# Both residual subtractions of the recurrent state's half 1 moved from VectorE to GpSimd

## The reference

```python
# layer 0: for each batch row, factors a1, b1, a2, b2 from gelu(LN(cond) @ W1 + bias1) @ W2 + bias2
mid = gelu(x @ base_down + (x @ a2) @ b2.T)
x   = x + (x + mid @ base_up.T + (mid @ b1) @ a1.T)
# layer 1: a recurrence over time, all batch rows together
xW = x @ Wx + b                      # (4, 512, 256)
h  = cond                            # (4, 256)
for t in range(512):
    h = tanh(xW[:, t] + h @ Wh)      # float32
    out[:, t] = x[:, t] + h
```

## Time and profile before

| | |
|---|---|
| Median of 3 runs | 555.61 us (550.74, 555.61, 555.97) |
| The profiled execution | 551.53 us, its span 549.7 us |
| TensorE busy | 511.1 us of the span (93%) |
| VectorE busy | 296.5 us (54%) |
| ScalarE busy | 176.5 us (32%) |
| GpSimd busy | 21.9 us (4%), none after 38.4 us |
| Tanh operations of the recurrence | 1024, from 54.2 to 544.9 us |

### The profile page before, as it was taken

How to read it: one execution, slowest core, us unless ns; L and a number is a source line. 1 busy time by engine, 2 the same in 40 slices (tenths; PEclk the granted TensorE clock), 3 DMA queues, 4 the chain that set the end, 5 groups by cost and what they waited for, 6 DMA issues and landing times.

```text
span 549.7 us, 32433 instructions
## 1 busy us (share of the span) xinstructions
PE 511.1 (93%) x14388; PEld 439.2 (80%) x14388; DVE 296.5 (54%) x2262; ACT 176.5 (32%) x1154; POOL 21.9 (4%) x34
## 2 busy tenths in 40 slices
PE   6988999999999999999998999899999989998995
PEld 4224777899999999999998888888888888888884
DVE  1154666555656555565555555555555555555553
ACT  2010222333333434333333333333333333333322
POOL 2850000000000000000000000000000000000000
PEclk7698999999999999999999999999999999999998
DMA  8950000000000000000000000000000000000000
GB/s 295 383 185 2 3 4 3 13 5 14 4 13 5 14 4 4 16 4 14 4 14 5 14 4 14 4 7 11 5 14 4 13 5 13 4 14 5 8 9 12
DMA packets 11346, 16.01 MB, mean 29 GB/s; under 512 B 1715, under 2 KB 7106, under 8 KB 11202
## 3 DMA queue, kind: packets, MB, share of 16 engines
q1 hardware_dynamic: 10352, 13.37, 7.4%
q10 hardware_dynamic: 854, 0.57, 0.4%
HBM read 11.85 MB, written 2.10 MB: 25 GB/s over the span
## 4 chain that ended last, share of the span: by engine, by line
PE 89%; ACT 5%; issue 2%; DVE 1%; DMA 1%; ACTq 0%; DVEq 0%
PE bank L833 65%; PE bank L762 7%; ACT w_sb L429 5%; PE bank L803 3%; PE bank L808 3%; PE bank L656 2%; PE bank L790 2%; PE bank L649 1%; DMA beta_sb<-in_L_cond_ln_beta 1%; PE bank L771 1%; PE bank L635 1%; PE bank L757 1%; PE bank L671 1%; PE bank L820 1%; PE bank L676 0%
## 5 line engine op out<-in xcount | busy, mean ns | idle before, releaser
L833 PE MATMUL bank<-w_sb,whp 128*128 128x52 bf16 x6132 | 243.0, 186 | 25.1 <-ACT w_sb L429 24.8
L591 DVE TENSOR_TENSOR r_ring<-w_sb 128x4 f32<-128x4 f32 x1022 | 136.5, 163 | 211.6 <-ACT w_sb L429 207.7
L429 ACT ACTIVATE w_sb<-bank 128x4 f32<-128x4 f32 x1024 | 142.0, 173 | 320.8 <-PE bank L833 320.8
L833 PEld LDWEIGHTS bank<-w_sb,whp 128*128 128x128 bf16 x6132 | 188.7, 96 | 68.4 <-ACT w_sb L429 46.4
L833 PE MATMUL bank<-r_ring,whp 128*128 128x52 bf16 x4096 | 219.9, 185 | 0.1
L833 PEld LDWEIGHTS bank<-r_ring,whp 128*128 128x128 bf16 x4096 | 173.9, 96 | 0.2 <-issue 0.2
L833 PE MATMUL bank<-l_ring,whp 128*128 128x52 bf16 (+1 forms) x2048 | 156.4, 177 | 0.0
L596 DVE TENSOR_TENSOR l_ring<-r_ring 128x4 bf16<-128x4 f32 x1024 | 136.3, 162 | 0.0
L833 PEld LDWEIGHTS bank<-l_ring,whp 128*128 128x128 bf16 x2048 | 121.6, 96 | 0.0
L762 PE MATMUL bank<-xp,wxp 128*128 128x32 bf16 x1536 | 71.6, 177 | 0.0
L762 PEld LDWEIGHTS bank<-xp,wxp 128*128 128x128 bf16 x1536 | 54.0, 96 | 0.0
(11 more groups left out here) (109 smaller groups left out, 192.3 us busy)
## 6 DMA issues: line engine op xcount, KB each, us to landing
w_sb<-in_L_cond_W SPq DMA_DIRECT2D x16, 512.0 KB, 10.8
x_sb<-in_x SPq DMA_DIRECT2D x4, 512.0 KB, 11.2
out<-o_sb SPq DMA_DIRECT2D x64, 32.0 KB, 1.6
down_sb<-in_L_cond_base_down SPq DMA_DIRECT2D x1, 256.0 KB, 5.2
w_sb<-in_L_cond_W ACTq DMA_DIRECT2D x1, 256.0 KB, 5.6
up_sb<-in_L_cond_base_up ACTq DMA_DIRECT2D x1, 256.0 KB, 9.0
wx_sb<-in_L_cond_Wx SPq DMA_DIRECT2D x1, 256.0 KB, 10.2
wh_sb<-in_L_cond_Wh SPq DMA_DIRECT2D x1, 256.0 KB, 10.4
```

Source lines behind the costliest of these rows:

```text
L429: nc.scalar.activation(h_ring[:, m, slot(pair, s), 0:B], zt, ACT.Tanh).then_inc(h_ready, 1)
L591: nc.vector.tensor_tensor(r_ring[:, k, q, 0:B], state_before(pair, s, k)[:, 0:B], state_hi_before(pair, s, k)[:, 0:B], ALU.subtract).then_ ...
L833: return nc.tensor.matmul(zbank(p, q, m)[:, col0:col0 + n], whp[part][:, k, P * m:P * (m + 1)], rhs[:, 0:n], start=False, stop=stop, skip_ ...
```

## The change

GpSimd gets a loop over all 512 steps with two subtractions each, r and l of half 1. VectorE keeps r and l of half 0 and its other work. Since two engines now count, `r_ready` and `l_ready` become one semaphore for each half, and TensorE's waits name them. No product, tanh, operand or shape is changed.

```diff
-        r_ready = sem("r_ready")
-        l_ready = sem("l_ready")
+        r_ready = [sem(f"r_ready{k}") for k in range(K2)]
+        l_ready = [sem(f"l_ready{k}") for k in range(K2)]
...
@@ gpsimd, after the memset of line 352 @@
+            def residues(pair, first, last):
+                for s in range(PAIR):
+                    q, step = s % 2, PAIR * pair + s
+                    pool.wait_ge(h_ready, 2 * step + 2)
+                    nc.gpsimd.tensor_tensor(r_ring[:, 1, q, 0:B], state_before(pair, s, 1)[:, 0:B],
+                                            state_hi_before(pair, s, 1)[:, 0:B], ALU.subtract).then_inc(r_ready[1], 1)
+                    pool.wait_ge(r_ready[1], step + 1)
+                    nc.gpsimd.tensor_tensor(l_ring[:, 1, q, 0:B], r_ring[:, 1, q, 0:B], r_hi[:, 1, q, 0:B],
+                                            ALU.subtract).then_inc(l_ready[1], 1)
+
+            over_pairs(residues)
...
@@ vector, residues @@
-                    for k in range(K2):
-                        dve.wait_ge(h_ready, 2 * PAIR * pair + 2 * s + k + 1)
-                        nc.vector.tensor_tensor(r_ring[:, k, q, 0:B], state_before(pair, s, k)[:, 0:B],
-                                                state_hi_before(pair, s, k)[:, 0:B],
-                                                ALU.subtract).then_inc(r_ready, 1)
-                    for k in range(K2):
-                        dve.wait_ge(r_ready, 2 * PAIR * pair + 2 * s + k + 1)
-                        nc.vector.tensor_tensor(l_ring[:, k, q, 0:B], r_ring[:, k, q, 0:B], r_hi[:, k, q, 0:B],
-                                                ALU.subtract).then_inc(l_ready, 1)
+                    step = PAIR * pair + s
+                    dve.wait_ge(h_ready, 2 * step + 1)
+                    nc.vector.tensor_tensor(r_ring[:, 0, q, 0:B], state_before(pair, s, 0)[:, 0:B],
+                                            state_hi_before(pair, s, 0)[:, 0:B], ALU.subtract).then_inc(r_ready[0], 1)
+                    dve.wait_ge(r_ready[0], step + 1)
+                    nc.vector.tensor_tensor(l_ring[:, 0, q, 0:B], r_ring[:, 0, q, 0:B], r_hi[:, 0, q, 0:B],
+                                            ALU.subtract).then_inc(l_ready[0], 1)
...
@@ tensor, recurrence @@
-                    pe.wait_ge(r_ready, done + 1)
+                    pe.wait_ge(r_ready[0], step + 1)
...
-                    pe.wait_ge(r_ready, done + 2)
+                    pe.wait_ge(r_ready[1], step + 1)
                     for part in range(2):
                         product(part, 1, 0, r_hi[:, 1, q, :])
-                    pe.wait_ge(l_ready, done + 1)
+                    pe.wait_ge(l_ready[0], step + 1)
                     product(0, 0, 0, l_ring[:, 0, q, :])
-                    pe.wait_ge(l_ready, done + 2)
+                    pe.wait_ge(l_ready[1], step + 1)
                     product(0, 1, 0, l_ring[:, 1, q, :], stop=True).then_inc(z_ready, 1)
```

More of the change, by code:

```diff
@@ L828, in recurrence @@
                     col0 = B * (s % TS // 2)
-                    done = 2 * PAIR * pair + 2 * s
+                    step = PAIR * pair + s
+                    done = 2 * step
                     def product(part, k, m, rhs, stop=False):
```

## The result

The changed kernel takes 629.64 us as the median of 4 runs (628.97 to 631.24), the kernel before 553.2 us beside it (550.74 to 555.97). The ratio is 1.138, 95% interval 1.134 to 1.143: slower by 14%. The profiled execution took 629.54 us, 78.0 more than the 551.53 before. The ratios in this document leave out executions that were longer at a lower granted clock; only the kernel with two more operations on VectorE had any, three of twelve, at 563 to 566 us.

What follows compares the result with a forecast made beforehand. It took a loop through three engines, 0.943 us a step, as the bound, with half 1's remainders lacking slack. 0.11 us in 478 steps plus twelve partly covered added 53 us to 555.6: 608 predicted, range 592 to 664.

Steps and rivals of the forecast that it cites:

- Rival 1: GpSimd's small subtractions take longer than 172 ns, at most 226 each: up to 104 us, 660; chance 0.18 including times between.
- two signs of being wrong: The GpSimd pair with hand-overs takes other than 0.50 us, or l of half 1 did not release the product.
- What releases the product: l of half 1 releases the product that ends output half 0, with no slack; the competing path is within 0.01 us.
- path B: Tanh of half 1, its r and l, then the 4-column product: 0.453 us from tanh's end, predicted 0.564, 0.11 longer.
- Less VectorE work is worth nothing: Two subtractions a step leave VectorE, 166 us of its 296.5 busy, but they stood in no queue: gain 0.
- The duration of GpSimd's operation: Each moved subtraction at 4 elements taken as 172 ns, bounded by 98 (memset) and 226 (float32 inputs).
- Hand-overs: Waits between operations: 0.08 us ahead of each GpSimd operation, against 0.035 on VectorE, and 0.06 from GpSimd to TensorE.
- The cover: Steps where other TensorE products hide the longer path: 21 early ones, twelve partly, one at the end; 478 pay fully.
- The sum: 478 steps at 0.11 us and twelve at about 0.06: 53 us added, 608.6 from the 555.6 median.
- Rival 2: VectorE and GpSimd hold each other off in SBUF for whole operations: +96 to +122 us, 652 to 678; chance 0.15.
- Rival 3: GpSimd's fixed cost is close to a memset's 98 ns, so not slower: 551 to 556 us; chance 0.04.
- Path A: TensorE's own queue of products from the tanh of half 0 to the 4-column product, 0.50 us; caps gain at 5 us.

## Why the prediction was right

The forecast was 608 us with a range of 592 to 664; measured was 629.64. Direction and mechanism were right, and one term of the sum was off. The result isn't in the forecast's own band (592 to 625, 0.56) but in "Rival 1 and between" (625 to 660, 0.18), and one of the two signs of being wrong did come: the pair of operations with its hand-overs takes 0.55 us, not 0.50. The range held because it took in that rival. The miss in added time is 25 us (53 forecast, 78.0 measured between the profiled executions). That the median is only 21.6 above 608 is luck: the sum started from 555.6, the median of three runs, and with a fourth it was 553.2. The bounds of the band mix two starts in the same way, 592 from the profiled 551.5 and 625 from the median.

- **What releases the product.** Right. "l of half 1 releases that product with no slack", and the cost followed path B by operation (0.080 and 0.078, together 0.158 of 0.160), by half, and went to zero where there was slack.
- **Less VectorE work is worth nothing.** Right: two more operations a step cost 0 to 3 us. Two steps of the first 41 did get 0.09 shorter (those with output sums ahead of the parts of layer 0), which is 0.2 us.
- **The duration of GpSimd's operation, "I take 172".** This is the mis-sized term. It measured 198 ns, between the value taken and the upper bound of 226. A line through 256 and 512 elements (the row of 256 is of 3 partitions) doesn't hold to 4: 198 ns at 4 elements, 331 at 64, 1152 at 512. Two operations, 0.052 us a step, 25 us in all, the whole of the miss. What GpSimd's fixed time is made of, no run shows.
- **Hand-overs, "0.08" twice and "0.06" to TensorE.** 0.077 to 0.079 and 0.057. Right, including the one from ScalarE that the trace of before didn't show.
- **The cover.** Right, and the count of 478 too. Most float32 steps are 1.31 to 1.32 us in both kernels. The first 41 steps grew by 3.0 us: 21 of them by about 0.16 (one by 0.27), less four that became 0.09 to 0.16 shorter. The twelve partly covered steps went from about 0.976 to 1.102.
- **The sum** with the measured terms: 0.157 x 478 = 75.0, plus 12 x 0.126 = 1.5 and 1 us of contention, 77.5 against 78.0 measured in the profiled executions.
- **Rival 1** (longer operations) was true in part. By rows it gave 660 at its bound.
- **Rival 2** (the engines hold each other off) had the right rule and the wrong size here. The Trainium skill, "SBUF — State Buffer", section "Who interferes with whom", says that a VectorE instruction with two SBUF inputs contends with a GpSimd instruction that reads SBUF; the traces agree (0.20 to 0.29 beside `x_res`, unchanged beside operations with one input in PSUM). That the second blocks for the whole of the first the small operations don't show: VectorE's l of half 0 starts 0.05 into GpSimd's r in each step and both keep their 163 and 198 ns. In the changed kernel, GpSimd's l starts 0.135 into `x_res`, of which 0.15 is left. Held until 0.057 behind the end of `x_res`, it ends only 0.015 later than it would have: 61 steps, with the one of 311 ns 1 us. In the kernel with l alone on GpSimd it starts 0.057 into `x_res`, and the same thing costs 8.4.
- **Rival 3** (not slower) would have needed 117 ns an operation. "Path A caps any gain at 5 us": it was 7.6 in the kernel without l of half 1. The slack of the two paths was put rightly (0.004 measured); the sum had nothing for the 0.009 that go away with the wait itself.

## What to carry to other kernels

Look for the wait that closes last and for the time by which the others miss it: here two paths were within 0.004 us, and one operation moved to a slower engine cost 40 to 46 us on one path and 1.5, within the noise, on another. Sharing a chain of dependent small operations between engines doesn't make it shorter; what counts is the number of hand-overs and the fixed cost of an operation on the engine that does them, and a line through large sizes underestimated that fixed cost here. An engine's busy share tells nothing of this: VectorE fell from 54% to 36% while the kernel got 14% slower, and rose to 67% at a cost of 0.3%, within the noise.

## What the runs showed of the hardware

- A GpSimd subtraction with two SBUF inputs over 128 partitions takes 198 ns at 4 elements, 331 at 64, 1152 at 512; VectorE's takes 163 at 4. An operation on GpSimd starts 0.077 us behind the end of what it waits for, on VectorE 0.034; TensorE's product starts 0.057 behind either.
- Beside a 0.284 us VectorE operation with two SBUF inputs, GpSimd's 128x4 operation that began after it ends 0.055 to 0.060 us behind that operation's end, if it would have ended sooner (0.064 to 0.070 beside the output sums, which come in pairs). One step of the changed kernel shows the same beside a VectorE copy of 0.29 us with one SBUF input (`b2s`, 32x256 float32): GpSimd's l took 311 ns and ended 0.058 behind it. So two inputs aren't the only case, though this copy comes only once in a run. Beside VectorE operations with one input in PSUM (380 and 415 ns) it keeps 198 to 200 ns.
- The other way: VectorE's 128x4 operation that started 0.09 into a 331 ns GpSimd operation ended 0.02 behind its end (0.26 us in place of 0.16).
- Two tanh operations over 128x4 can start 0.070 us apart on ScalarE.
- At a granted clock of 1.00, TensorE's product behind one that had to wait follows it by 0.038 us, otherwise by 0.025; the tanh that waits for the 4-column product starts 0.214 behind its start if it had to wait, 0.204 if not.
